# Adjacency as int8 in DRAM, fetched a row tile ahead, and the self projection of a batch kept in SBUF: a graph layer with residual and layer norm

## The reference, cut to what matters

```python
mi = einsum('bkd,od->bko', x, W[:, :512])      # self projection,      x is 8 x 2048 x 512 fp32
mj = einsum('bkd,od->bko', x, W[:, 512:])      # neighbour projection
a = adj.astype(float32)                        # 2048 x 2048, int32 zeros and ones, shared by all batches
deg = a.sum(axis=1)
y = x + deg[None, :, None] * (mi + b) + einsum('ij,bjo->bio', a, mj)
out = (y - mean(y)) / sqrt(var(y) + 1e-5)      # over the last axis, 512 wide
```

## Time and profile before

| | |
|---|---|
| median of 3 runs | 1652.01 us (1650.88 to 1652.76) |
| time of the profiled execution | 1651.12 us |
| its span, first to last instruction | 1649.3 us, TensorE's mean granted clock 0.999 |
| PE busy | 1639.2 us (99%) |
| DVE, ACT, POOL busy | 850.8, 661.6, 500.4 us |

### The profile page before, as it was taken

One profiled execution on the slowest core, in us unless ns is written; L12 is line 12 of the kernel. 1 busy time (PEld: TensorE's weight loads), 2 busy tenths in 40 slices (PEclk: granted clock), 3 DMA queues, 4 the chain that ended last, 5 costly groups with the idle time before them and its releaser, 6 DMA issues.

```text
span 1649.3 us, 24823 instructions
## 1 busy us (share of the span) xinstructions
PE 1639.2 (99%) x7212; PEld 1347.9 (82%) x7212; DVE 850.8 (52%) x1878; ACT 661.6 (40%) x964; POOL 500.4 (30%) x386
## 2 busy tenths in 40 slices
PE   9999999999999999999999999999999999999998
PEld 6788888888888888888888888888888888888886
DVE  8768644555444444455444445445444445444544
ACT  5655334423354224533245322453325522255221
POOL 2431234311343113431144311442114421154210
PEclk9999999999999999999999999999999999999999
DMA  6667423333223332243322432233323243232432
GB/s 205 197 189 228 158 77 101 123 109 100 86 92 127 114 95 83 96 133 102 95 91 93 134 109 85 92 102 125 111 83 99 91 136 105 76 102 83 128 114 70
DMA packets 102698, 187.26 MB, mean 114 GB/s; under 512 B 11408, under 2 KB 11408, under 8 KB 102672
## 3 DMA queue, kind: packets, MB, share of 16 engines
q1 hardware_dynamic: 84816, 154.44, 29.6%
q10 hardware_dynamic: 17856, 32.51, 6.4%
HBM read 119.80 MB, written 67.11 MB: 113 GB/s over the span
## 4 chain that ended last, share of the span: by engine, by line
PE 95%; DVE 2%; DMA 1%; issue 1%; ACT 0%; SPq 0%; DVEq 0%; ACTq 0%
PE agg_ps L362 55%; PE cross_ps L330 13%; PE main_ps L338 13%; PE main_ps L340 13%; DMA adj_in<-in_adjt 1%; DVE deg_part L580 0%; DVE W_lo L530 0%; DVE W_df L533 0%; DMA mi_in<-in_wt 0%; DMA mi_dram<-mi 0%; PE deg_ps L347 0%; DMA out<-r 0%; ACT cross L441 0%; DVE adjT L527 0%; DVE stats L602 0%
## 5 line engine op out<-in xcount | busy, mean ns | idle before, releaser
L362 PE MATMUL agg_ps<-mj_hi,adjT 128*128 128x512 f32 x2048 | 797.0, 389 | 0.0
L362 PE MATMUL agg_ps<-mj_lo,adjT 128*128 128x512 f32 x2048 | 796.7, 389 | 0.0
L457 ACT ACTIVATE adjT<-adjT 128x2048 fp32r (+1 forms) x128 | 245.3, 1916 | 548.4 <-PE agg_ps L362 548.3
L362 PEld LDWEIGHTS agg_ps<-mj_lo,adjT 128*128 128x128 f32 x2048 | 384.5, 188 | 79.7
L362 PEld LDWEIGHTS agg_ps<-mj_hi,adjT 128*128 128x128 f32 x2048 | 384.4, 188 | 79.7
L338 PE MATMUL main_ps<-W_hi,x_hi 128*128 128x512 f32 x1008 | 392.5, 389 | 1.5 <-DVE mi L566 1.5
L340 PE MATMUL main_ps<-W_lo,x_lo 128*128 128x512 f32 x1008 | 392.2, 389 | 0.0
L279 POOL TENSOR_TENSOR mi_in<-mi_in,bias 128x512 f32<-128x512 f32 x128 | 166.4, 1302 | 651.3 <-DMA mi_in<-mi_dram 651.3
L330 PE MATMUL cross_ps<-W_df,x_df 128*128 128x512 f32 x1008 | 270.8, 390 | 0.2
L273 POOL TENSOR_TENSOR mj_lo<-mj,mj_hi 128x512 f32 (+1 forms) x126 | 169.6, 1346 | 271.6 <-ACT mj_hi L445 271.6
L600 DVE TENSOR_TENSOR r<-agg_ps,r 128x512 f32<-128x512 f32 x128 | 88.5, 691 | 315.2 <-PE agg_ps L362 315.2
(11 more groups left out here) (59 smaller groups left out, 607.3 us busy)
## 6 DMA issues: line engine op xcount, KB each, us to landing
mi_dram<-mi SPq DMA_DIRECT2D x128, 256.0 KB, 2.1
mi_in<-mi_dram SPq DMA_DIRECT2D x128, 256.0 KB, 2.7
r<-in_x SPq DMA_DIRECT2D x128, 256.0 KB, 2.7
out<-r SPq DMA_DIRECT2D x128, 256.0 KB, 2.1
x_raw<-in_xt ACTq DMA_DIRECT2D x124, 256.0 KB, 2.8
adj_in<-in_adjt SPq DMA_DIRECT2D x64, 256.0 KB, 3.1
r<-in_wt SPq DMA_DIRECT2D x4, 256.0 KB, 5.5
adj_in<-in_xt SPq DMA_DIRECT2D x2, 256.0 KB, 3.9
```

The source lines that it names most:

```text
L362: last = nc.tensor.matmul(agg_ps[s][:, :], adjT[s][:, j, :], part[:, j, :], start=(j == 0 and part is mj_hi), stop=(j == NT - 1 and part i ...
L457: nc.scalar.activation(adjT[s][:, :, :], adjT8[:, :, bass.ds(i * P, P)], ACT.Copy).then_inc(adjT_ready, 1)
```

## The change

- `adjT8` (2048 bytes times 16 in each partition) is gone. ACT casts a chunk into one of four small tiles `chunk8`, waits for its own cast, and issues a transfer that stores it to `adj_dram`, laid out by row tile: the 512 bytes of a partition go to four places, 128 bytes each. Before it casts chunk c it waits for the store of chunk c-4.
- SP loads one row tile of int8, 2048 bytes a partition, into one of two buffers `adj8` (`load_adj8`). The load of tile i+2 stands in SP's program behind the store of output tile i-1 and ahead of the load of `r` for tile i+3. The last two steps of a batch load the first two tiles for the next. `widen` now waits for this load.
- `mi` has 16 tiles. The projection writes tile t, POOL adds the bias in place, the residual reads it there. `store_mi`, `load_mi`, `mi_in` and the wait of `combine_mi` for the last store are gone, and `add_bias` waits only until its tile has been projected.
- In the aggregation phase of batch 0 the 32 remaining chunks are taken four a step in steps 1 to 8 (before: 3, 3, 3, 3, 2, 2, 4, 4, 4, 4 in steps 1 to 10), and the third sum of counts (`degrees(2)`) stands ahead of step 5 on PE instead of step 7.
- The scratch and staging tiles of the start are taken from `mi` instead of `adjT8` and `mi_in`, with whole rows of 512 in place of two halves of 256.

```diff
-        mi_dram = nc.dram_tensor("mi_dram", [TILES, P, DO], fp32, kind="Internal").ap()
-        adjT8 = sb("adjT8", [P, NT, N], i8)
+        adj_dram = nc.dram_tensor("adj_dram", [NT, P, NT, P], i8, kind="Internal").ap()
+        adj8 = [sb(f"adj8{s}", [P, NT, P], i8) for s in range(2)]
+        chunk8 = [sb(f"chunk8{s}", [P, DO], i8) for s in range(4)]
...
-        mi = sb("mi", [P, DO], fp32)
-        mi_in = [sb(f"mi_in{s}", [P, DO], fp32) for s in range(2)]
+        mi = sb("mi", [P, NT, DO], fp32)
...
-        AGG_CHUNKS = [0, 3, 3, 3, 3, 2, 2, 4, 4, 4, 4, 0, 0, 0, 0, 0]
+        AGG_CHUNKS = [0, 4, 4, 4, 4, 4, 4, 4, 4, 0, 0, 0, 0, 0, 0, 0]
...
-            def store_mi(n):
-                sp.wait_ge(mi_ready, n + 1)
-                sp.dma_start(mi_dram[n], mi[:, :]).then_inc(mi_stored, 16)
...
+            def load_adj8(i, s, zero):
+                if zero:
+                    done = NT * (i // TPB + 1)
+                    for w in range(4):
+                        sp.wait_ge(adj_stored[w], 16 * (done // 4))
+                sp.dma_start(adj8[s][:, :, :], adj_dram[i]).then_inc(adj8_loaded[s], 16)
...
-                        if not (ending and u >= GT - 2):
-                            sp.wait_ge(res_ready, m + 1)
-                            load_mi(m + 2, u)
+                        wraps = ending and u >= GT - 2
+                        if not (last_batch and wraps):
+                            sp.wait_ge(adjT_ready, m + 1)
+                            load_adj8(u - 2 if wraps else i + 2, u % 2, zero and not wraps)
...
-            def add_bias(m, u, turn):
-                pool.wait_ge(mi_loaded[u % 2], turn)
-                pool.tensor_tensor(mi_in[u % 2][:, :], mi_in[u % 2][:, :], bias[:, :], ALU.add).then_inc(mib_ready, 1)
+            def add_bias(m, i):
+                pool.wait_ge(mi_ready, m + 1)
+                own = mi[:, bass.ds(i, 1), :].rearrange("p t d -> p (t d)")
+                pool.tensor_tensor(own, own, bias[:, :], ALU.add).then_inc(mib_ready, 1)
...
-                        if i == 7:
+                        if i == 5:
                             degrees(2)
...
                 act.wait_ge(adj_loaded[s], 16 * (c // AB + 1))
-                nc.scalar.activation(adjT8[:, j, q * DO:(q + 1) * DO], adj_in[s][:, :], ACT.Copy).then_inc(adj_cast, 1)
+                if c >= 4:
+                    act.wait_ge(adj_stored[w], 16 * (c // 4))
+                nc.scalar.activation(chunk8[w][:, :], adj_in[s][:, :], ACT.Copy).then_inc(adj_cast, 1)
+                act.wait_ge(adj_cast, c + 1)
+                act.dma_start(adj_dram[TPB * q:TPB * (q + 1), :, j, :].rearrange("t p i -> p t i"),
+                              chunk8[w][:, :].rearrange("p (t i) -> p t i", t=TPB)).then_inc(adj_stored[w], 16)
...
-            def widen(i, s, chunks):
-                if chunks is not None:
-                    act.wait_ge(adj_cast, chunks)
-                nc.scalar.activation(adjT[s][:, :, :], adjT8[:, :, bass.ds(i * P, P)], ACT.Copy).then_inc(adjT_ready, 1)
+            def widen(s, turn):
+                act.wait_ge(adj8_loaded[s], turn)
+                nc.scalar.activation(adjT[s][:, :, :], adj8[s][:, :, :], ACT.Copy).then_inc(adjT_ready, 1)
...
-            def combine_mi(n):
+            def combine_mi(n, t):
                 dve.wait_ge(main_done, 2 * n + 2)
                 dve.wait_ge(cross_ready, 2 * (n - NATIVE) + 2)
-                dve.wait_ge(mi_stored, 16 * n)
```

More of the change, by code:

```diff
@@ L86, in bass_adj_resnorm @@
         deg_ps = pb("deg_ps")
-        w_stage = [r[0], r[1], r[2], r[3], mi_in[0], mi_in[1], deg_part, mi]
-        scratch = [adjT8[:, 2 * q:2 * q + 2, N // 2:N].bitcast(fp32) for q in range(NT // 2)]
-        w_top = scratch
+        w_stage = [r[s][:, :] for s in range(4)] + [mi[:, NT - 3, :], mi[:, NT - 2, :], deg_part[:, :], mi[:, NT - 1, :]]
+        w_top = [mi[:, 4 + q, :] for q in range(2 * DK)]
         x_first = [adj_in[2][:, :].bitcast(fp32), adj_in[3][:, :].bitcast(fp32)]
-        def halves(ap):
-            return ap.rearrange("p (a d) -> p a d", a=2)
         w_loaded = [sem(f"w_loaded{c}") for c in range(2 * DK)]
@@ L114, in bass_adj_resnorm @@
         mi_ready = sem("mi_ready")
-        mi_stored = sem("mi_stored")
-        mi_loaded = [sem(f"mi_loaded{s}") for s in range(2)]
+        adj_stored = [sem(f"adj_stored{s}") for s in range(4)]
+        adj8_loaded = [sem(f"adj8_loaded{s}") for s in range(2)]
         r_loaded = [sem(f"r_loaded{s}") for s in range(GT)]
@@ L204, in batch @@
                 zero = known(bt) and bt == 0
+                last_batch = known(bt) and bt == NB - 1
                 base = NT * bt
[L207 to L220, removed]
+                if zero:
+                    for t in range(NT):
+                        for c in proj_chunks(t):
+                            load_chunk(c + AB)
+                        if t == 10:
+                            for i in range(2):
+                                load_adj8(i, i, True)
+                    sp.wait_ge(w_ready, 2 * DK)
                 for u in range(GT - 1):
@@ L300, in batch @@
                     for u in range(2):
-                        add_bias(NT * bt + 2 * k + u, u, 16 * (NP * bt + k + 1))
+                        add_bias(NT * bt + 2 * k + u, 2 * k + u)
             over_batches(pool, batch)
@@ L314, in project_native @@
                         pe.wait_ge(w_loaded[c], 16)
-                    last = nc.tensor.matmul(into[:, :], x_first[n][:, k * P:(k + 1) * P], w_stage[c][:, :],
+                    last = nc.tensor.matmul(into[:, :], x_first[n][:, k * P:(k + 1) * P], w_stage[c],
                                             start=(k == 0), stop=(k == DK - 1))
@@ L411, in copy_w_hi @@
                 act.wait_ge(w_top_ready, order + 1)
-                nc.scalar.activation(halves(W_hi[:, c, :]), w_top[order], ACT.Copy).then_inc(w_hi_ready, 1)
+                nc.scalar.activation(W_hi[:, c, :], w_top[order], ACT.Copy).then_inc(w_hi_ready, 1)
             def native_mj_hi(n):
@@ L420, in native_mi @@
                 act.wait_ge(main_done, NATIVE + n + 1)
-                if n:
-                    act.wait_ge(mi_stored, 16 * n)
-                nc.scalar.activation(mi[:, :], (main_ps if n == 0 else cross_ps)[1][:, :],
+                nc.scalar.activation(mi[:, n, :], (main_ps if n == 0 else cross_ps)[1][:, :],
                                      ACT.Copy).then_inc(mi_ready, 1)
@@ L498, in proj @@
                         if last_group and u in (0, 2):
-                            widen(u // 2, u // 2, NT if zero else None)
+                            widen(u // 2, 16 * (NP * bt + 1))
                 over_groups(act, zero, True, proj)
@@ L507, in batch @@
                             act.wait_ge(agg_done, i + 1)
-                            widen(i + 2, i % 2, NT * ((i + 2) // TPB + 1))
+                            widen(i % 2, 16 * ((i + 2) // 2 + 1))
                         root(i)
@@ L514, in batch @@
                             act.wait_ge(agg_done, m + 1)
-                            widen(2 * k + i + 2, i, None)
+                            widen(i, 16 * (NP * bt + k + 2))
                             root(m)
@@ L526, in split_w @@
                 dve.wait_ge(w_loaded[c], 16)
-                nc.vector.tensor_scalar(top.bitcast(u32), halves(w_stage[c][:, :]).bitcast(u32),
+                nc.vector.tensor_scalar(top.bitcast(u32), w_stage[c].bitcast(u32),
                                         HI_BITS, None, ALU.bitwise_and).then_inc(w_top_ready, 1)
                 dve.wait_ge(w_top_ready, order + 1)
-                nc.vector.tensor_tensor(halves(W_lo[:, c, :]), halves(w_stage[c][:, :]), top,
+                nc.vector.tensor_tensor(W_lo[:, c, :], w_stage[c], top,
                                         ALU.subtract).then_inc(w_lo_ready, 1)
                 dve.wait_ge(w_lo_ready, order + 1)
-                nc.vector.scalar_tensor_tensor(halves(W_df[:, c, :]), top, 1.0 / S,
-                                               halves(W_lo[:, c, :]).bitcast(fp32),
+                nc.vector.scalar_tensor_tensor(W_df[:, c, :], top, 1.0 / S,
+                                               W_lo[:, c, :].bitcast(fp32),
                                                ALU.mult, ALU.subtract).then_inc(w_ready, 1)
@@ L647, in proj @@
                                 count_chunk(c)
-                        combine_mi(n)
+                        combine_mi(n, t)
                         if zero:
```

17 lines of the change are left out of this document (6 added, 11 removed).

## The result

The changed kernel takes 1662.73 us (median of 4 runs, 1662.32 to 1663.66), the kernel before took 1651.75 beside it: ratio 1.0066, 95% interval [1.0054, 1.0078]. It is slower by 11 us. The prediction was 1660.9 us, and slower.

What follows compares the result with a forecast made beforehand. PE bounds the kernel, busy 1639.2 of 1649.3 us, with at most 2.4 us of waits to regain. Terms -1.5 (`mi`) - 0.9 (counts) + 1.3 (casts) + 10.0 (late DVE) = +8.9 gave 1660.9 us, range 1654 to 1674.

Steps and rivals of the forecast that it cites:

- The train holds DVE: Batch 0 aggregation: POOL's 16 bias additions run back to back and hold DVE's two-SBUF-input operations, 9.5 us.
- The tightness of 0.5 us: Batch 0, 48th count: DVE done at 137.8 even without contention, PE there at 137.3, so 0.5 us too little.
- Adjacency through DRAM, steady state: Aggregation steps: the adjacency load lands just before ACT widens, and PE has 5.3 us in hand; 0 us.
- Where PE waits: Batch 0: the 10.0 us of waiting is spread ahead of steps 3 and 4 and the sum of counts before step 5.
- The final scaling: DVE's last normalisation operation in batch 0: may wait 0 to 1.3 us beside POOL, as no row shows it.
- ACT's casts: Batch 0 projection: ACT waits for its own cast, +0.52 us a chunk, making `x_df` late for PE; +1.3 us.
- -1.5 - 0.5 + 1.3 = -0.7: Batch 0 projection: -1.5 from PE's wait for `mi`, -0.5 from that ahead of `degrees(0)`, +1.3 from ACT's casts.
- Degrees(3): Batch 0 aggregation: the 64th count comes by step 9, needed at step 11, so PE's 0.4 us wait is given back.
- Later batches, 0 us: Batches 1 to 7: no counts, the train adds three or four waits of 1.3 us, covered by 6.5 us; 0 us.
- Pieces of 128 bytes: Batch 0 adjacency stores: ACT's issue taken as 0.4 us; queues full in steps 1 to 8, but DVE sets the pace.
- The rival of dear pieces: Small pieces cost more in ACT's issue or the queues: slower still, 1671 to 1697, mostly up to 1675; chance 18%.
- 16 ns a piece: Batch 0 steps with four chunks: queue time left for each 128-byte piece; a piece was taken near that.

Runs made afterwards that it cites:

- Run 1: The changed kernel with each POOL bias addition in batch 0 held until the residual two tiles before is done; 1655.09 us, ratio 1.0023 against the kernel before.
- run 8: The changed kernel with every POOL bias addition made twice, the first into an unused tile, a train of 32; 1708.82 us, ratio 1.035.
- run 9: The changed kernel with paced additions and, in batch 0, ACT's square root ahead of the widening; 1651.46 us, ratio 1.0008.
- run 2: The changed kernel with POOL's bias additions cut to one column of each tile, as early and in the same order; 1655.47 us, ratio 1.0027.
- run 4: The changed kernel, train kept, with `degrees(2)` ahead of step 6 and chunks 4, 4, 4, 2, 2, 4, 4, 4, 4; 1660.81 us, 1.0050.
- Run 3: The changed kernel with 14 and 17 idle products on PE ahead of step 3 and ahead of `degrees(2)`; 1659.61 us, ratio 1.0055.
- run 6: The changed kernel with paced additions and each chunk's store issued by ACT behind the next chunk's cast; 1656.8 us, ratio 1.0038.
- run 7: The changed kernel with paced additions, stores issued one cast later, and `degrees(2)` a step later; 1652.43 us, ratio 1.0006.

## Why the prediction was right, and where not

The whole is right: slower, 1662.7 against 1660.9, by the mechanism named. Step by step:

- *The train holds DVE*: right. Predicted was a hold of 9.5 us on top of 0.5 us of tightness, and the 48th count at 147.3; it ends at 146.5. PE would have been there at 137.3, so the lateness is 9.2 against 10.0. Run 1 took away 7.6 us of time by spreading the additions, run 8 added 46 by doubling them. The sum can be redone from the trace, with the free durations of run 9: DVE starts at 107.6 and not at 108, its own work takes 29.1 us and not 29.8, and the train adds 9.2 us and not 9.5. The parts of the 9.2 are further off: residuals 2.0 (forecast 1.9), one-column operations 1.4 (1.3), scaling 0.9 (0 to 1.3), the first four counts 3.8 (5.2), the next residual 1.0 (1.3). That they add up so well is partly luck: a held operation took less than assumed, and the train lasted until 126.8 and not 122.2.
- *The tightness of 0.5 us* was none: without the train and with the root in time DVE would have been done at 107.6 + 29.1 = 136.8, before PE at 137.3.
- *The step that failed* is the 0 us of "Adjacency through DRAM, steady state". It was right for batches 1 to 7, but in batch 0 the first load of a tile came late for ACT, and I priced the widening for PE alone. Behind it in ACT's order stood the table load and the square root for which DVE waited. In the changed kernel that made DVE 0.6 us late (0.83 us of idling at the first root, where 0.27 is usual), since the train had it busy meanwhile. Without the train it made 1.8 us in run 1 and 2.2 in run 2, most of what they waited. Run 9 moved the root and took the wait from 2.35 to 0.72.
- *Where PE waits*: ahead of step 3 as forecast (the sum is read from 125.60 to 126.28, forecast 125.6 to 127.4) and ahead of `degrees(2)`, but not at step 4. DVE had read the sum of step 2 by 133.5, and PE, at full clock, would not have come to step 4 before. In run 4, where the clock stayed up, PE waits there 0.68 us, but for the widened tile.
- *The missing term*, and the largest error, is the clock: it was put at nothing. A wait was priced at its own length; a wait of 3.9 us also cost 3.4 us of slow products behind it. Run 3 gave back 3.1 us of time by filling the idle stretches.
- *The final scaling*, left at 0 to 1.3 us: it is held, 1.48 against 0.55, so 0.9.
- *ACT's casts*, +1.3: the mechanism is right, the size is not. The rows show 1.5 us of idling for `x_df`, but each such stop costs PE some 0.3 us more than its row, as the starts of the cross products show: the four tiles with a wait take 6.0, 6.0, 6.4 and 6.1 us where 5.44 is the yardstick, 2.8 us together. The waits for `mi` and ahead of `degrees(0)` were likewise worth more than their 2.0 us, again 2.8. So the projection phase was forecast at -1.5 - 0.5 + 1.3 = -0.7 and came out at +0.1. The start of the program has little part in it: PE waited 1.1 us for the weights in the profiled execution and 0.2 before, but by 22 us the two kernels are only 0.14 us apart.
- *Degrees(3)*, -0.4: right.
- *Later batches, 0 us*: right for the change. DVE was busy 102.8 us in a stretch of 200 us behind batch 0 and 97.6 in the same stretch before, so the trains hold it there too, without a wait of PE. That cover ends between a train of 16 and one of 32 (run 8), and it ends at ACT's widening, where I had looked for 6.5 us of slack at DVE's sum.
- *Pieces of 128 bytes*: ACT's store is issued in 0.38 to 0.44 us, as taken (the rows that I read at 0.3 to 0.4 for transfers of 256 KB show 0.38 to 0.47, which changes nothing). The rival of dear pieces is refuted for the issue: the stores land 3.1 us after issue in the median, and no cast waits for one. The queues are indeed full in the steps with four chunks, share 0.90 to 1.06 in the windows from 130 us on, as the forecast with 16 ns a piece had it; what a piece took was not measured. They set no pace: in run 9 the share is as high and PE is busy nearly throughout.

In numbers: projection phase +0.8 against the forecast, lateness -0.8 (9.2 for 10.0), clock behind `degrees(2)` +3.4; together +3.4 over +8.9, that is 12.3, against the 12.0 of the spans. The first two errors cancel, which is luck. As a share of the whole time the forecast is 0.1% off; as a share of the change it gave 8.9 of 11.0 us, and nearly all that it lacks is the clock. Run 3 gives most of it back (3.1 us of the 3.4).

What stays open: why the second `r` comes up to 1.4 us late (0.31, 0.84 and 1.41 us in runs 1, 2 and 9), whether by the queues' load or by the adjacency load ahead of it, was not tried. Nor was it tried why the clock stays up behind some waits.

## What to carry to other kernels

A buffer in SBUF in the place of a round trip through DRAM also removes the pacing that the loads gave to the work behind them; if that work runs on POOL beside DVE, pace it again by hand, one operation for each that DVE completes. When a load moves a widening, look at everything that stands behind it in that engine's order, here a square root on which the critical engine waited. And price a new wait of PE of some microseconds at more than its length: the lower clock behind it may cost as much again.

## What the runs showed of the hardware

- PE's idle stretches of 3.87, 3.33 and 2.35 us (changed kernel, run 1) were each followed by a stretch at the lower clock, of some 7, 4 and 3 us, and so were those of 2.58 us in run 2 and 2.72 in run 4; those of 2.08 and 1.58 us in the profiled executions of runs 6 and 7 were not, nor was the one of 3.32 us in run 4. The length of the idling alone does not tell it, and the mean clock of executions of one kernel differs (0.996 to 0.999 in run 6).
- A DVE scaling with one wide SBUF input and two one-column operands was held by POOL's addition (1.48 us for 0.55), as was a cast with one input (L569, 1.51 for 0.42).
- The store of 64 KB in pieces of 128 bytes was issued in 0.38 us, about as one of 256 KB (0.33 to 0.43), and landed in 3.1 us (medians of the changed kernel).
